# Attention scores as three half-precision products, from high and low parts that ScalarE and VectorE cut

## The reference, cut to what matters

```python
q = (x @ Wq).reshape(N, S, HEADS, HEAD_DIM).transpose(0, 2, 1, 3)      # k, v alike
logits = jnp.einsum('nhid,nhjd->nhij', q, k) * scale                    # scale = 1/8
logits = logits + causal[None, None, :, :]
attn = jax.nn.softmax(logits, axis=-1)
out = jnp.einsum('nhij,nhjd->nhid', attn, v)
```

## Time and profile before

| | us |
|---|---|
| Time, median of 3 runs (lowest, highest) | 979.01 (975.36, 981.52) |
| Time of the profiled execution | 979.85 |
| Its span | 978.6 |
| Of it self-attention, to the last turned probabilities | 380 |
| PE busy over the span | 889.2 (91%) |
| DVE, ACT, POOL busy | 613.6 (63%), 554.1 (57%), 342.0 (35%) |
| L521 (scores): records of matmuls, busy, mean | 512, 60.0, 353 ns |

### The profile page before, as it was taken

How to read it: one execution, slowest core, us unless ns; L and a number is a source line. 1 busy time by engine, 2 the same in 40 slices (tenths; PEclk the granted TensorE clock), 3 DMA queues, 4 the chain that set the end, 5 groups by cost and what they waited for, 6 DMA issues and landing times.

```text
span 978.6 us, 23292 instructions
## 1 busy us (share of the span) xinstructions
PE 889.2 (91%) x8118; PEld 679.6 (69%) x8118; DVE 613.6 (63%) x1634; ACT 554.1 (57%) x1333; POOL 342.0 (35%) x456
## 2 busy tenths in 40 slices
PE   3899999999999998999999997798969999999980
PEld 2678878787777886666666665565647887888860
DVE  3456566655555554557776766799736666666653
ACT  3667756565555665556555653687725554555543
POOL 1333333332323432324433332347822233223233
PEclk9999999999999999999999999899979999999995
DMA  9900000000000000400100000347752322333326
GB/s 329 274 16 1 2 2 2 1 2 1 2 1 2 2 2 1 51 1 22 44 23 1 2 1 1 131 150 257 250 163 62 54 47 45 51 50 46 48 24 183
DMA packets 61117, 57.44 MB, mean 59 GB/s; under 512 B 19727, under 2 KB 56783, under 8 KB 60879
## 3 DMA queue, kind: packets, MB, share of 16 engines
q1 hardware_dynamic: 51039, 43.07, 15.3%
q0 software_dynamic: 7152, 9.34, 5.9%
q10 hardware_dynamic: 2816, 3.54, 1.0%
HBM read 37.13 MB, written 18.82 MB: 57 GB/s over the span
## 4 chain that ended last, share of the span: by engine, by line
PE 30%; POOL 10%; issue 8%; DVE 8%; ACT 3%; DMA 2%; DVEq 0%; POOLq 0%; ACTq 0%
PE ps L1960 11%; PE ps L1968 7%; PE ps L31 6%; POOL rows_x L1644 5%; PE ps L1969 3%; POOL dl L1347 2%; POOL sqs L1334 1%; DMA back_y<-slots,dst 1%; PE ps L337 1%; PE ps L1951 1%; POOL an L1351 1%; DVE t L1453 1%; DVE dl L1465 1%; DVE xs_row L865 1%; ACT hn L1263 1%
## 5 line engine op out<-in xcount | busy, mean ns | idle before, releaser
L1960 PE MATMUL ps<-slots,e 128*128 128x128 f16 x1872 | 191.0, 221 | 4.6 <-DVE slots L2092 2.3
L447 POOL TENSOR_SCALAR prob<-prob,rden 128x128 f32<-128x128 f32 (+1 forms) x256 | 104.0, 425 | 230.4 <-DVE rden L702 230.2
L1960 PEld LDWEIGHTS ps<-slots,e 128*128 x1872 | 154.1, 99 | 37.8 <-issue 6.2
L1928 POOL DMA_INDIRECT back_y<-slots,dst x39 | 67.5, 1730 | 173.6 <-ACT slots L2044 163.3
L1968 PE MATMUL ps<-e,sw 128*128 x312 | 117.9, 380 | 1.3 <-DVE sw L2082 1.3
L617 ACT ACTIVATE prob<-prob,nmx 128x128 f32<-128x128 f32 (+1 forms) x256 | 114.1, 452 | 4.3 <-DVE nmx L695 4.3
L2031 ACT ACTIVATE slots<-slots 128x512 f32<-128x512 f32 x78 | 49.1, 630 | 101.4 <-DVE slots L2077 101.4
L31 PE MATMUL ps<-s,whh 128*128 128x512 f16 x432 | 105.0, 378 | 0.0
L31 PE MATMUL ps<-xT,wqkv 128*128 128x256 f16 x768 | 98.4, 279 | 5.6 <-DVE wqkv L683 5.6
L31 PEld LDWEIGHTS ps<-xT,wqkv 128*128 128x128 f16 x768 | 71.2, 100 | 26.6 <-issue 16.9
L695 DVE CUSTOM_DVE_ANT_0 prob<-ps,mask 128x128 f32<-128x128 f32 (+1 forms) x256 | 80.4, 352 | 13.2 <-PE ps L521 13.2
(11 more groups left out here) (241 smaller groups left out, 1855.0 us busy)
## 6 DMA issues: line engine op xcount, KB each, us to landing
e<-in_L_ffn_ew SPq DMA_DIRECT2D x18, 512.0 KB
piece<-in_L_ffn_ew SPq DMA_DIRECT2D x12, 512.0 KB
rows_x<-zrow SPq DMA_DIRECT2D x1, 5031.0 KB, 19.0
xg<-rows_x SPq DMA_DIRECT2D x39, 128.0 KB, 2.5
piece<-in_L_ffn_sh_w SPq DMA_DIRECT2D x4, 512.0 KB
back_y<-xT SPq DMA_DIRECT2D x4, 512.0 KB, 3.9
out<-xs_row SPq DMA_DIRECT2D x8, 256.0 KB, 2.1
xs_row<-in_x SPq DMA_DIRECT2D x1, 1536.0 KB, 17.9
```

Of the source, the lines that this page charges most:

```text
L447: PO.tensor_scalar(prob[m % 3][:, h, r], prob[m % 3][:, h, r], rden[m % 2][:, h, t:t + 1], 1.0, ALU.mult, ALU.mult).then_inc(normed, 1)
L1928: PO.indirect_dma_start(back_y, bass.IndirectOffsetOnAxis(ap=dst[:, i:i + 1], axis=0), yo[i % 2], None, compute_op=ALU.add).then_inc(rows_ ...
L1960: yield PE.matmul(ps[:, 2 * u + q, (k % 4) * P:(k % 4) * P + P], w[ch][h], xgT[u][j][:, ch, :], start=n == 0, stop=n == 3 * DC - 1)
```

## The change

Bank 0 is now read twice. ACT makes the high part of queries and keys together, in one instruction over 512 columns, scaled by the root of the scale and rounded to half precision. DVE makes the low part, bank times scale minus the high part, also in one instruction over 512 columns (`queries_and_keys_low`). The scores are three half-precision matmuls for each 32-bit one, 12 for an item in place of 4, still with 64 rows. The next `project_qk` waits for the low part, and so do the scores. A semaphore that nothing waited for (`ident_cut`) is gone, and this changes no order.

```diff
-            qk = [sb(c, f"qk{i}", [P, 2, S]) for i in range(2)]
+            qk = [[sb(c, f"qk{i}{u}", [P, 2, S], F16) for i in range(2)] for u in range(2)]
...
                     if n >= 1:
-                        PE.wait_ge(qk_out, 2 * n)
+                        PE.wait_ge(qk_lo, n)
...
-                    PE.wait_ge(qk_out, 2 * (m + 1))
+                    PE.wait_ge(qk_hi, m + 1)
+                    PE.wait_ge(qk_lo, m + 1)
...
-                            mm = PE.matmul(ps[:, 2 + h, query_tile(t)], qk[m % 2][r, 0, t * P:t * P + P],
-                                           qk[m % 2][r, 1, 0:(t + 1) * P], start=True, stop=True)
+                            q = [w[r, 0, t * P:t * P + P] for w in qk[m % 2]]
+                            k = [w[r, 1, 0:(t + 1) * P] for w in qk[m % 2]]
+                            mm = split_matmuls(PE, ps[:, 2 + h, query_tile(t)], [(q, k)])
...
-                    SC.mul(qk[n % 2][:, 0, :], ps[:, 0, 0:S], SCALE / WS).then_inc(qk_out, 1)
-                    SC.mul(qk[n % 2][:, 1, :], ps[:, 0, S:2 * S], 1 / WS).then_inc(qk_out, 1)
+                    SC.mul(qk[n % 2][0][:, :, :], ps[:, 0, :].rearrange("p (k t) -> p k t", k=2),
+                           QK_SCALE).then_inc(qk_hi, 1)
...
+                def queries_and_keys_low(n):
+                    VE.wait_ge(qk_hi, n + 1)
+                    VE.scalar_tensor_tensor(qk[n % 2][1][:, :, :], ps[:, 0, :].rearrange("p (k t) -> p k t", k=2), QK_SCALE,
+                                            qk[n % 2][0][:, :, :], ALU.mult, ALU.subtract).then_inc(qk_lo, 1)
...
                     if 0 <= j < ITEMS and j % 2 == 0:
                         values_out(j)
+                    if j + 2 < ITEMS:
+                        queries_and_keys_low(j + 2)
                     share = share_at(j - 1)
```

More of the change, by code:

```diff
@@ L54, in decoder_layer @@
     SCALE = float(HD) ** -0.5
+    QK_SCALE = SCALE ** 0.5 / WS
     XSCALE = float(D) ** -0.5
@@ L112, in decoder_layer @@
         const_fill, const_cut, const_ve = sem("const_fill"), sem("const_cut"), sem("const_ve")
-        ident_cut = sem("ident_cut")
         zeroed = sem("zeroed")
@@ L143, in constants_half @@
             for i in range(2):
-                VE.tensor_scalar(identh[i][:, :], ident[:, :], LOW if i else 1.0, None, ALU.mult).then_inc(ident_cut, 1)
+                VE.tensor_scalar(identh[i][:, :], ident[:, :], LOW if i else 1.0, None, ALU.mult)
         bih = sb(top, "bih", [P, 6])
@@ L330, in vw_tensor @@
             elif i == 1:
-                PE.wait_ge(qk_out, 2 * ITEMS)
+                PE.wait_ge(qk_lo, ITEMS)
             elif i == 2:
@@ L375, in decoder_layer @@
                 sem(k) for k in ("qk_mm", "v_mm", "s_mm", "p_turned", "o_mm", "y_mm"))
-            qk_out, v_out, masked, exped = (sem(k) for k in ("qk_out", "v_out", "masked", "exped"))
+            qk_hi, qk_lo, v_out, masked, exped = (sem(k) for k in ("qk_hi", "qk_lo", "v_out", "masked", "exped"))
             recip, normed, pT_out, o_hi, o_lo = (
```

## The result

| | before | after |
|---|---|---|
| Time, median, us (lowest, highest) | 978.78 (975.36, 981.52) | 994.6 (992.09, 995.1) |
| Profiled execution, us; its span | 979.85; 978.6 | 995.1; 993.9 |
| Ratio of the times, 95% interval | 1 | 1.0161 (1.0129 to 1.0193) |
| PE busy, DVE busy over the span, us | 889.2, 613.6 | 883.6, 654.9 |

The times are of four executions each. The kernel became 15.8 us slower, not 5.9. The direction was right, but the size is 2.7 times the forecast. That 994.6 still lies in the range that was given (to 995) is luck: its upper end was drawn for rival one and for a part of the clock's, and rival one did not come true. The profiled executions differ by 15.3.

What follows compares the result with a forecast made beforehand. PE was taken to bound self-attention. Scores -5.5, late copies +11.2 and start +0.2 gave +5.9 us on 979.85, so 985.8 us; likeliest case 983 to 990, range leaving out 2 in 10 981 to 995.

Steps and rivals of the forecast that it cites:

- rival one: Scores on PE: matmuls run in program order, one head blocks the other, no gain; 991.3 us, chance 0.15.
- the clock's: PE behind late copies in steps 27 and 51: idle time drops the clock to half, 989.2 us; chance 0.07.
- the gain of the scores: Self-attention on PE: scores end earlier in 42 ordinary steps, 0.13 us each, 5.5 us gained.
- the late copies: DVE's copy of the probabilities, for which PE waits, comes late in eleven steps: 11.2 us lost.
- the floor of 0.61: Self-attention, PE bound: weighing of values starts no sooner than 0.61 us after the probabilities' copy starts; ordinary steps took 0.74.
- The scores on PE: Both heads run side by side; score records end about 0.67 us after their start, gaining 0.13 per ordinary step.
- Rivals one and two: The second, on PE's scores: half-precision products of 64 rows do not overlap at all; 1001 us, chance 0.08.
- The low part on DVE: New DVE instruction takes 0.69 us, waits for ACT in odd steps, shifts the queue by 1.33; eleven steps lose 11.2.
- The six steps with `inputs_low`: Self-attention: the probabilities' copy there waits for L675, which waits for ACT, hiding the low part; no gain or loss.
- Rival three: Half-speed clock on PE behind late copies: 989.2 us with two falls, 994 with all five steps; chance 0.07.
- Start: Steps 0 to 2 of self-attention: the low part comes just behind, costing 0.2 us.
- Not slower: DVE's queue: ACT's high part ready when DVE's masks end, shift 0.61 instead of 1.33; 978.2 us, chance 0.06.

Runs made afterwards that it cites:

- The low part alone: Kernel before with its 32-bit scores, plus one DVE low-part instruction per item that scores and next projection wait for: 999.71 us, ratio 1.0231.
- the move behind the share: Changed kernel with the low part placed after the preparation share in odd steps 17 to 51: 979.9 us, ratio 1.0008.
- the variant for the transposes only: Changed kernel with the low part placed after the preparation share only in steps 21, 29, 37 and 45: 986.23 us, ratio 1.0083.

## Why the prediction was wrong in size

The prediction put two costs at nothing and they came: the wait of the transposes in four of the steps with `inputs_low`, 4.4 us, and the clock, 6.4 us. Its two large terms, the gain of the scores and the late copies, were right to 0.1 us each.

- **What bounds, and the floor of 0.61:** right. The ordinary steps moved from 0.74 to 0.61, and the gain was limited by the copy, not by the products.
- **The scores on PE:** right. 0.68 in records where about 0.67 was expected. Rivals one and two fell: three products of one head, then three of the other, overlap fully here, and alternating them changes nothing. By rival one's order the group would have been about 1.0 long, its 0.77 and the 0.27 of the last record. That order is the rule of the Trainium skill, page "TensorE: Matmul & The Clock Gate", section "Part 3: Packing small matmuls", that matmuls start and end strictly in the order of the program. For matmuls on different rows of the array the measurement decides against the rule.
- **The low part on DVE:** right, to 0.02 a step: 0.692 mean for L703, 0.597 for ACT's copy, eleven late copies for 11.1 us. The low part alone and the move behind the share showed that the loss comes with this instruction, and that 14.7 us of it go with its place and the wait there.
- **The six steps with `inputs_low`, "they neither gain nor lose":** wrong for four of them, 4.4 us. I followed the copy behind L675 and left out the wait that stands in front of the transposes on PE. It depends on the preparation share, whose end I had just moved by 1.33. The trace of before had the hint, a wait of L483 for L287 of 0.2 us in step 45: a race won by nothing in the kernel before. The term should have been 4 x (1.33 less the slack of the share before the transposes).
- **The clock, "so probably not":** wrong, 6.4 us. I had compared two idle times, 3.38 with the clock lost and 2.78 with the clock kept, with the new one of 2.5, and gave this rival 0.07. The others, which came out at 1.8 to 2.0, I had not worked out. It fell behind idle times of 1.80, 2.03, 2.50 and 2.56. The price was near: 1.6 for each, 1.7 expected. Filling the idle time gave 5.9 back. Rival three, with falls in all five steps, worked out to 994. Four came, and it is the transposes' 4.4 that bring the time up to that number: the match is luck.
- **Start, "I put 0.2":** 1.0 in this pair of traces. The first scores came 0.84 later than before (21.76 for 20.92): the low part starts there when the high part is done, at 20.92, and PE waits for it; I had looked at the second scores only. How much of this is left at the third weighing stays open, since that one moves by as much as 0.98 between two kernels with the same code there.
- **Not slower:** its condition, that DVE finds the high part ready, is what the move behind the share brought about in the steps with a share, and its 978.2 came near the 979.9 measured there. The tails of steps 11 and 59 have no share, and the copies behind them still came 1.0 late each.

## What to carry to other kernels

When an instruction is put into the middle of an in-order queue behind a wait, list every signal that the rest of that queue gives, not only the one that is late today; each is a race that may have been won by a tenth of a microsecond. Put such an instruction behind work that is ready and in front of work that is not urgent: beside the same kernel without it, the same 0.69 us in each step cost 22.6 us in all at one place and 7.9 one place later. And price idle time on TensorE twice, once as waiting and once as the half-speed stretch that may follow.

## What the runs showed of the hardware that was not expected

- The clock does not follow from the length of one idle time. In the changed kernel it fell to 0.50 behind 1.80, 2.03, 2.50 and 2.56 us of idle time and stayed behind 1.78; in the kernel with the low part alone it stayed behind 2.31 and 2.37 and fell behind 1.84; in the variant for the transposes only, it stayed behind 2.03, 1.81, 1.78 and 2.56 and fell behind 2.50; with the heads alternating it fell behind 2.51, 1.81 and 1.78 and stayed behind 2.04 and 2.56. So idle times that are the same to 0.01 went either way, and the 6.4 us are those of one execution. Behind the 1.61 and less that the variant with the low part behind the share has in these steps no fall was seen. What decides between them is open; no run here tells it.
- Two heads on different halves of the array's rows go through twelve half-precision products side by side, in whichever order they are written: 0.67 and 0.68 us, where one head's six would need 0.50 by their starts and 0.27 less 0.11 for the end of the last record, 0.66, by the rows of other products before the change.
